# Gate and up projections of token-tile pairs as seven half-width products in a fused attention and feed-forward kernel

## The reference, cut to what matters

```python
def act_quant(x):                      # per token, per block of 128 columns
    amax = max(abs(xb)); scale = amax / 448.0 + 1e-12
    return xb / scale, scale
def linear_dsv3(x, wq, w_scale):       # weight scale per 128 x 128 block
    xdq = act_quant(x) multiplied back by its scale
    wdq = wq * w_scale
    return xdq @ wdq.T
...
g = linear_dsv3(xf, w1, w1_scale)      # xf: 1024 x 512, w1, w3: 1792 x 512
u = linear_dsv3(xf, w3, w3_scale)
h = jax.nn.silu(g) * u
y = linear_dsv3(h, w2, w2_scale)       # w2: 512 x 1792
...
x = x + _layernorm(_L0_attn_ref(_layernorm(x), ...))
x = x + _layernorm(_L0_ffn_ref(_layernorm(x), ...))
```

## Time and profile before

| | us |
|---|---|
| median of 3 runs (1111.95 to 1113.28) | 1112.96 |
| the profiled execution | 1111.28 |
| its span, first to last instruction | 1109.5 |

### The profile page before, as it was taken

One profiled execution on the slowest core, in us unless ns is written; L12 is line 12 of the kernel. 1 busy time (PEld: TensorE's weight loads), 2 busy tenths in 40 slices (PEclk: granted clock), 3 DMA queues, 4 the chain that ended last, 5 costly groups with the idle time before them and its releaser, 6 DMA issues.

```text
span 1109.5 us, 16613 instructions
## 1 busy us (share of the span) xinstructions
PE 1088.5 (98%) x5134; PEld 908.3 (82%) x5134; DVE 858.3 (77%) x1740; ACT 674.9 (61%) x1320; POOL 768.8 (69%) x765
## 2 busy tenths in 40 slices
PE   9999999999999999999999999999999999999997
PEld 7888888888888888888888888888887778888885
DVE  5635566667899899989999999997687966666666
ACT  6533233327989798888788898885677532222215
POOL 6844447537768878869799799787845755666635
PEclk9999999999999999999999999999999999999999
DMA  6444474455889899898998989984210133333422
GB/s 231 129 176 152 150 235 138 143 152 199 293 296 344 291 317 336 287 346 281 319 353 305 319 313 319 339 277 154 97 58 1 38 115 119 119 109 84 121 64 98
DMA packets 163537, 227.86 MB, mean 205 GB/s; under 512 B 37761, under 2 KB 126465, under 8 KB 158593
## 3 DMA queue, kind: packets, MB, share of 16 engines
q1 hardware_dynamic: 163456, 226.88, 60.9%
HBM read 130.50 MB, written 96.34 MB: 204 GB/s over the span
## 4 chain that ended last, share of the span: by engine, by line
PE 86%; DVE 5%; POOL 2%; ACT 2%; DMA 2%; issue 1%; POOLq 0%; DVEq 0%; SPq 0%
PE psS L1636 24%; PE psT L1636 16%; PE psOY L1636 16%; PE psOY L1773 15%; PE psOY L1788 14%; PE psT L1754 2%; DMA p_scr_long<-probs_long 1%; DVE y L1429 1%; DMA squares_long<-p_scr_long 1%; DVE oT_lo L1284 1%; ACT probs_long L1065 1%; PE psS L1648 0%; POOL x L893 0%; POOL qT_lo L687 0%; DVE squares_long L1371 0%
## 5 line engine op out<-in xcount | busy, mean ns | idle before, releaser
L1065 ACT ACTIVATE probs_long<-probs_long,negmax 128x896 f32<-128x896 f32 (+9 forms) x124 | 122.2, 987 | 6.4 <-DVE negmax L1352 6.0
L687 POOL TENSOR_TENSOR pT_lo<-squares_long,pT_hi 128x896 fp32r<-128x896 f32 (+3 forms) x47 | 108.2, 2309 | 25.2 <-ACT pT_hi L1060 25.0
L748 POOL TENSOR_SCALAR probs_short<-probs_short,rsum 128x256 f32<-128x256 f32 (+9 forms) x128 | 75.9, 605 | 47.9 <-DVE rsum L1359 47.7
L815 POOL TENSOR_SCALAR hidden<-mask,hr,hs 128x128 f32<-128x128 f32 x112 | 49.2, 449 | 85.2 <-DVE hr L1449 85.2
L1788 PE MATMUL psOY<-wd_hi,oT_hi 128*128 128x512 f32 x256 | 103.5, 404 | 2.2 <-DVE oT_lo L1284 1.8
L1371 DVE STREAM_TRANSPOSE squares_long<-squares_long 128x1792 f32<-128x1792 f32 (+3 forms) x54 | 101.6, 1882 | 0.9 <-DMA squares_long<-p_scr_long 0.9
L1114 ACT ACTIVATE mask<-psS 128x256 f32<-128x256 f32 x56 | 21.5, 383 | 130.8 <-PE psS L1636 130.8
L1788 PE MATMUL psOY<-wd_hi,oT_lo 128*128 128x512 f32 x256 | 100.2, 391 | 0.0
L1788 PE MATMUL psOY<-wd_lo,oT_hi 128*128 128x512 f32 x256 | 100.1, 391 | 0.0
L1636 PE MATMUL psS<-kT_hi,qT_hi 128*128 128x512 f32 (+5 forms) x280 | 98.2, 351 | 1.3 <-DVE negmax L1352 0.7
L748 POOL TENSOR_SCALAR probs_long<-probs_long,rsum 128x896 f32<-128x896 f32 (+9 forms) x70 | 74.6, 1068 | 33.2 <-DVE rsum L1359 32.9
(11 more groups left out here) (216 smaller groups left out, 3389.4 us busy)
## 6 DMA issues: line engine op xcount, KB each, us to landing
q_raw<-q_scr SPq DMA_DIRECT2D x64, 256.0 KB, 5.1
p_scr_long<-probs_long SPq DMA_DIRECT2D x14, 896.0 KB, 5.7
squares_long<-p_scr_long SPq DMA_DIRECT2D x14, 896.0 KB, 6.9
p_scr_long<-probs_long SPq DMA_DIRECT2D x12, 1024.0 KB, 6.0
squares_long<-p_scr_long SPq DMA_DIRECT2D x12, 1024.0 KB, 6.8
p_scr_long<-probs_long SPq DMA_DIRECT2D x14, 768.0 KB, 5.5
squares_long<-p_scr_long SPq DMA_DIRECT2D x14, 768.0 KB, 4.4
raw<-in_w_qk SPq DMA_DIRECT2D x10, 1024.0 KB, 6.3
```

The source lines that it names most:

```text
L687: return nc.gpsimd.tensor_tensor(dst, source, hi.bitcast(F32), ALU.subtract)
L748: nc.gpsimd.tensor_scalar(row, row, rsum[:, column(t, u)], 1.0, ALU.mult, ALU.mult).then_inc(p_ready[lane(t)], 1)
L815: last = nc.gpsimd.tensor_scalar(to, columns_of(h_sb[:, m % 2, b * P:(b + 1) * P], to), hr[:, m % 2, b:b + 1], hs[:, m % 2, b:b + 1], ALU. ...
L1065: nc.scalar.activation(row, row, ACT.Exp, bias=negmax[:, column(t, u)], scale=-1.0, accum_out=lsum[:, column(t, u)]).then_inc(e_done[lane( ...
```

## The change

In chunks 2 to 6 the gate and up of two neighbouring token tiles (2p and 2p + 1) is computed with seven products instead of eight. The 2 x 2 blocks are: two token tiles, two halves of the 512 input features (two slices each), and gate and up as the two column halves. Seven products of sums of row blocks (S1 to S4, A11, A12, A22, B11...) with sums of weight blocks (T1 to T4, B11, B21, B22) are made, each two slices of three matmuls, 256 columns wide, and added up. Chunks 0 and 1 stay as they were.

- **PE**: for a pair, five products, `down` of tile n - 4, the products P2 and P3 (added in PSUM onto P1 and P5), `down` of tile n - 3. That is 42 matmuls of 256 columns in place of 24 of 512. Six PSUM banks are used in turn.
- **DVE**: five additions of 128 x 256 per pair (`sum_of_products`). Per token pair, once, in chunk 1: four sums of activation blocks of 128 x 256 (`half_sums`) and a low part of 128 x 1024 (`low_of_half`); for the last pair the fp32 activations are first added up again from their parts. The work of two tiles is written in one sequence.
- **ACT**: a copy of P1 per pair (`copy_first`); the silu of the even tile reads the sum `gate_early`, that of the odd tile reads PSUM. Scaling of weights moves here from POOL as instructions of 128 x 128, four to a piece, six pieces to a chunk (L1204). High parts of the weights are nine casts instead of six. In chunk 1, four casts of 128 x 1024 (`hi_of_half`). In chunk 0, six more copies of 128 x 512 (`x32`).
- **POOL**: per chunk four sums of weight blocks and nine low parts, in place of six scalings and six low parts.
- **SP**: `load_down` is issued at the second tile of a chunk, `load_up` at the seventh, both behind `hidden_back`; `hidden_away` and `hidden_back` keep their order.
- The loops are written out on all engines.

The diff, cut to its core:

```diff
@@ SP
-            with sp.Fori(0, (C - 3) // 2) as r:
...
-            for n in range((C - 2) * NT, C * NT - LAST_TURNS):
+            for n in range(NT, C * NT - LAST_TURNS):
+                c, i = n // NT, n % NT
                 hidden_away(n, n)
                 hidden_back(n - 1, 16 * ((n - 1) // 2 + 1))
+                if i == 1 and FIRST_W <= c < C - 1:
+                    load_down(c + 1)
+                if i == KT + 2 and c < C - 2:
+                    load_up(c + 2)
@@ POOL
+            POOL_WORK = {1: ("T1",), 2: ("T3", "T2"), 3: ("T4", "B11"), 4: ("B21", "B22"), 5: ("T3", "T1"), 6: ("T2", "T4"),
+                         7: ("D0", "D1")}
...
+                    if c < C - 1 or i < NT - 1:
+                        quantise_hidden(c * NT + i, c * NT + i)
+                    if c < C - 1:
+                        for name in POOL_WORK.get(i, ()):
+                            if name[0] == "T" and i <= 3:
+                                sum_of_weights(c + 1, name)
+                            else:
+                                low_of_weights(c + 1, name)
@@ ACT
+            def scale_piece(c, k):
...
+                for j in range(BANK // P):
+                    block_ = source[:, j * P:(j + 1) * P]
+                    last = nc.scalar.activation(block_, block_, ACT.Copy, scale=table[:, col + j:col + j + 1])
+                last.then_inc(piece_scaled, 1)
...
+            for n in range(NT, 2 * NT):
                 silu_gate(n, n % 2)
+                prepare(FIRST_W, n - NT)
+                if n % 2:
+                    hi_of_half(n // 2 - NT // 2)
+                hi_of_hidden(n - LAG + 1, n - LAG + 1)
+            for n in range(FIRST_W * NT, C * NT, 2):
+                c, i = n // NT, n % NT
+                copy_first(n)
+                prepare(c + 1, i)
+                hi_of_hidden(n - LAG + 1, n - LAG + 1)
+                silu_early(n)
+                prepare(c + 1, i + 1)
...
+                hi_of_hidden(n - LAG + 2, n - LAG + 2)
...
+                silu_late(n + 1)
@@ DVE
+            for n in range(NT, FIRST_W * NT):
+                turn_hidden(n - LAG + 1, n - LAG + 1, loads_of(n - LAG + 1))
+                make_hidden(n, n % 2)
+                lo_of_hidden(n - LAG + 1, n - LAG + 1)
+                add_down(n - LAG, (n - LAG) % NT)
+                p = n // 2 - NT // 2
+                if n % 2 == 0:
+                    half_sums(p)
+                else:
+                    low_of_half(p)
@@ PE
+            for n in range(FIRST_W * NT, C * NT, 2):
+                c, i = n // NT, n % NT
+                if i == 0:
+                    pe.wait_ge(up_ready, ready_blocks(c))
...
+                for name in W_ORDER[:5]:
+                    half_product(n, name)
...
+                next_down(n - LAG)
+                half_product(n, "P2")
+                half_product(n, "P3")
+                next_down(n + 1 - LAG)
```

More of the change, by code:

```diff
@@ L475, in turned_units @@
             return blocks.rearrange("p k (u a q) -> p u k a q", u=len(units), a=HG)
+        FIRST_W, COPIED = 2, NT - 2
+        ffn_banks = [psS[:, k // 2, k % 2 * BANK:(k % 2 + 1) * BANK] for k in range(4)] + [psT[:, k, :] for k in range(2)]
+        W_ORDER = ("P1", "P6", "P7", "P5", "P4", "P2", "P3")
+        W_SUMS = ("both", "three", "up_early", "gate_early", "up_late")
+        T_ORDER, HI_ORDER = ("T1", "T3", "T2", "T4"), ("B11", "B21", "B22", "T3", "T1", "T2", "T4", "D0", "D1")
+        HALF_ORDER = ("S3", "S1", "S2", "S4")
@@ L1224, in _, with prepare @@
                     norms(*item)
[L1226 to L1232 removed]
+            ACT_WORK = {0: (0, 1), 1: (2, 3), 2: ("B11", "B21"), 3: ("B22", "T3"), 4: ("T1", "T2"), 5: ("T4", KT), 6: (KT + 1, "D0"),
+                        7: ("D1",)}
+            def prepare(c, i):
+                for name in ACT_WORK[i] if c < C else ():
+                    if isinstance(name, int):
+                        scale_piece(c, name)
+                    else:
+                        hi_of_weights(c, name)
             def square_last(s):
```

332 lines of the change are left out of this document (224 added, 108 removed).

## The result

The changed kernel takes **1198.39 us** (median of 4 runs, 1197.36 to 1202.81) against 1112.94 before: 1.0776 times as long, 95% interval 1.0758 to 1.0794. The sign was forecast; the size was not: 1170 was predicted, and the time lies 4 us above the range of 1138 to 1194. The profiled execution's span is 1196.3 us, 86.8 longer than before, where the working had 57.5.

A forecast was written before the change was run, and what follows sets the result against it. PE was taken to bound the kernel before, a ring through DVE, POOL and DMA after. Chunk 0 +0.5, chunk 1 +10, chunks 2 to 5 +46, chunk 6 +3.3, tail -2.3: +57.5, forecast 1170 us, range 1138 to 1194.

The forecast's parts named there:

- PE's term: TensorE, per pair of tiles: 7.76 us instead of 8.16 with 256-column matmuls 0.12 apart, 8 us less over 20 pairs.
- The ring: Turn, hidden products, quantise, store and bring back form a loop within one pair: 8.96 us against PE's 7.76.
- T3: Tile 3 of a prepared chunk: ACT's cast waits for POOL's sum and delays the low part, +3.4, pair 12.4 us.
- Low parts between two quantises: Tile 4: POOL's low parts B21 and B22 stand between the pair's two quantises, +1.45, pair 10.4 us.
- scalings on ACT: Tile 1: eight scalings stand between the even silu and the turned tile's high part, +1.1, pair 10.05 us.
- The start of a chunk: Pair from tile 6: low parts T2 and T4 +1.45, PE's late start +0.4, load beside transfers +0.6; 11.4 us.
- S + 5.9: 5.9 us after DVE starts turning tile n - 2 (S), weights are ready and PE starts the next chunk.
- Chunk 1: DVE's half sums and low parts, waits for ACT, and DVE waiting for POOL: +10 us, bounds 4 and 18.
- rival C: DVE locked out by POOL at a pair's second product: +20 us over 19 pairs, 1190 us; chance 0.09.
- Chunk 0: Six copies on ACT ahead of the low part of the activations: +0.5 us, between 0 and 3.7.
- Chunk 6: Nothing is prepared there: three intervals of about 9.27 us for 24.5 before, +3.3 us.
- the loops: Loops written out on all engines: 0, within 1 us either way.

The follow-up runs named there:

- the best order that was tried: Changed kernel with DVE's turn behind both hidden products of a pair, weight preparation moved earlier and the load at the fifth tile; all work kept: 1149.2 us.

## Why the prediction was wrong

Step by step, in its own order:

- **What bounds before, and PE's term: right.** 256 columns are 0.12 apart at the full clock, a pair is 7.80 on PE against 7.76 worked out. What failed is that the distance was taken as 0.12 everywhere: in the changed kernel it was 0.21 for 13 to 28 matmuls in nine places from chunk 2 on.
- **The ring: right.** Opened in two places that have nothing else in common, the first and third pairs of a chunk fell from 10.1 to 11.9 us to 8.2 to 9.5, most of them to 8.3 to 8.8. Bare it was 9.6 to 9.9 in the run with POOL's weight work cut and 9.1 to 10.2 in chunk 6; 8.96 is a little low. The 3.60 from store to turn held: 1020.21 to 1023.84 in that run.
- **T3, the largest term and the one that rested on no row: right.** 12.4 worked out, 12.6 to 13.0 measured, and 2.8 us gone when it alone was moved.
- **Low parts between two quantises, scalings on ACT: the sizes fit**, 10.5 to 11.8 for 10.4 and 10.1 to 11.9 for 10.05. With POOL's weight work cut the third pair fell to 9.6 to 9.9 and the first stayed at 10.1 to 10.3; the scalings were not taken out alone. The first three pairs of chunks 2 to 5 are together 6.1 us above the working.
- **The start of a chunk: the step that failed.** 11.4 worked out, 14.6, 14.3, 14.5, 13.6 measured: 11.4 us of the 29 that are missing. I had written that PE starts at S + 5.9, and it did (turn at 1135.26, first product at 1141.24). But I went on with the five products at 0.12 us each. Nothing in the trace of before shows PE after a long wait at this place, because PE never waited there; but the working itself leaves it idle there for at least 3.6 us (11.4 less 7.76), and I did not ask what that does. For all 30 matmuls of the five products the other clock costs 30 x (0.21 - 0.12) = 2.7 us; it was 2.6 at the start of chunk 6. The second part is the load. In the kernel before, 11.6 us passed from its issue to the first scaling; the change issues it a tile later and scales at the chunk's first tile, on ACT, so that a wait of 3.0 us stands ahead of a high part and a silu. I priced the eight scalings and what the load does to the hidden transfers (+0.6), and not the wait for the load itself. At the starts of chunks 3 to 5 the load is the longer of the two, at that of chunk 6 the clock is all. With both removed the starts are 11.1 to 11.4.
- **Chunk 1: mis-sized.** +10 worked out with bounds 4 and 18, +16.1 measured. Nearly half of that, 7.5, lies in its last pair (15.7), which holds the start of chunk 2: PE's first product there starts at 946.35, 0.1 behind the end of POOL's last low part of the weights, and 13 matmuls follow at the lower clock. What the earlier trace rows show is there too: half sums were taken at 0.36 us; beside POOL they are 1.5, and in the whole chunk DVE's half sums, low parts and scales are stretched by some 8 us. How much of this lengthened the chunk is not shown: with the half sums back at 0.41 the second and third pairs fell by 0.2 and 1.3 only. The Trainium skill (SBUF — State Buffer, "SBUF: two separate sides") has it so: a DVE instruction with two SBUF inputs and one of GpSimd that reads SBUF shut each other out, whichever is first. The trace agrees in both directions: 0.41 against 1.51 above, and POOL's sum takes 2.26 instead of 1.26 at 917.16, behind a low part of DVE that began at 916.93. I had given that rule as rival C with 0.09, for the second product of a pair in chunks 2 to 6, where it takes 0.42 to 0.60. Other instructions of DVE are held there: 6 of 32 low parts take 0.67 to 1.55 instead of 0.40, 8 of 32 scales 0.66 to 0.95 instead of 0.17, 11.5 us in the four chunks with the products. My own sign for C, over 1 us, was seen in some of them. What it costs in this order is not separated; in the order with the weights early, POOL's weight work cost a chunk 1.1 to 2.5 us.
- **Chunk 0: mis-sized.** +0.5 worked out, with 3.7 as its upper bound, +4.0 measured, some 2 of it the copies. Part of it looks like the same shutting out: the low part waited for the copy and came 0.26 us later, and with it the scale met POOL's scaling that it had just missed; in the run without the copies it takes 0.17 again, and the four behind it 1.94. DVE's timeline before:

```profile
859.34 0.17 DVE L1418 TENSOR_SCALAR qs<-amax 128x4 f32<-128x4 f32 x1
859.76 1.90 DVE L1429 TENSOR_SCALAR y<-y,qr,qs 128x128 f32<-128x128 f32 x4
```

  And in the changed kernel:

```profile
859.62 0.75 DVE L1546 TENSOR_SCALAR qs<-amax 128x4 f32<-128x4 f32 x1
860.62 3.10 DVE L1557 TENSOR_SCALAR y<-y,qr,qs 128x128 f32<-128x128 f32 x4
```

- **Chunk 6, the last pair, the end, the loops: right** within 1.1 us each.
- **The range.** Its upper end was rival C alone. What is missing (starts +11, chunk 1 +6, first three pairs +6, chunk 0 +3.5, the rest +2) all lies on one side: waits and a lower clock that the schedule laid out by hand had left out. Bounds of single terms were at hand for 8 more in chunk 1 and 3 more in chunk 0, and adding these to the middle alone would have reached 1181, with C 1201.

Where did the gain go, then? PE saves 0.36 us a pair, 7 us over 20 pairs. In the best order that was tried it does not come out: the pair is 8.4 to 10.0, and even without POOL's weight work 8.2 to 9.6, where PE alone needs 7.80. What holds it above that is open beyond POOL's part. And in every version tile 16 comes 18 to 26 us later than before, for what chunks 0 and 1 do to get ready. Of the 37 us that the best order is longer than before, 19 lie ahead of tile 16, 14 in chunks 2 to 5 and the rest behind. No version with seven products came below the kernel before, and a saving of 7 us on PE could not have paid for the 18.

## What to carry to other kernels

Where a change shortens the engine that bounds, lay out one period by hand on all queues and ask whether a loop closes in it: who waits for the store of what comes later in the same period. Where your own layout leaves the matmul engine idle for some us, price what it does next at both clocks. And when work moves to another engine, move its waits along with it: count the time from the issue of a load to its first reader before and after, and look at who stands behind that reader.
